# Keys and values of the fourth attention projected during the third feed-forward, four tiles at a time

## The reference

```
x = x + tanh(g_ffn[2])   * L2_ffn(layernorm(x))                  # the third feed-forward
x = x + tanh(g_xattn[3]) * L3_xattn(layernorm(x), ctx, ctx)      # the fourth attention

L2_ffn(x):     h = gelu(quant(x) @ quant(w_fc).T + b_fc)         # 128 -> 512, blocks of 32 share an exponent
               return quant(h) @ quant(w_proj).T + b_proj        # 512 -> 128
L3_xattn(q,k,v): q,k,v = q@Wq+bq, k@Wk+bk, v@Wv+bv               # 16 heads of 8
               return softmax(q k^T / sqrt(8)) v @ Wo + bo
```

## Time and profile before

| | |
|---|---|
| time, three runs | 1069.31, 1070.88, 1072.28 us; median 1070.88 |
| profiled execution | span 1084.4 us, 30129 instructions; no other time of it is given |
| busy | PE 898.7 us (83%), DVE 885.9 (82%), ACT 686.2 (63%), POOL 523.1 (48%) |
| mean granted PE clock | 0.898 |
| mask of attention 1 taken by DVE (L1896) | at 148.8 us |

### The profile page before, as it was taken

The page is one execution under the profiler, slowest core; times in us unless marked ns, Lnnn a source line. Parts: engine busy times, 40 slices in busy tenths (PEclk is TensorE's granted clock), DMA queues, the critical chain, the costliest instruction groups (busy, mean ns, idle before and its releaser), DMA issues.

```text
span 1084.4 us, 30129 instructions
## 1 busy us (share of the span) xinstructions
PE 898.7 (83%) x11539; PEld 707.4 (65%) x11557; DVE 885.9 (82%) x2296; ACT 686.2 (63%) x1794; POOL 523.1 (48%) x612
## 2 busy tenths in 40 slices
PE   8999999999999932999689999978899999434443
PEld 5888889978887721566457778834478888222222
DVE  6999888878999961567568889889978888899997
ACT  6888864377776610444447777866678888555553
POOL 6444412254367676223287787255553332355554
PEclk9999999999999966899889999988899999655665
DMA  8760000000000012365111111000000000000000
GB/s 214 186 241 2 3 2 2 1 2 3 3 24 27 27 46 76 114 187 175 51 33 32 26 31 29 6 1 2 1 2 2 2 3 3 1 10 16 15 15 24
DMA packets 60526, 44.42 MB, mean 41 GB/s; under 512 B 15196, under 2 KB 55781, under 8 KB 59366
## 3 DMA queue, kind: packets, MB, share of 16 engines
q1 hardware_dynamic: 55718, 34.09, 10.6%
q0 software_dynamic: 4096, 8.34, 2.7%
q10 hardware_dynamic: 576, 0.13, 0.1%
HBM read 23.73 MB, written 18.87 MB: 39 GB/s over the span
## 4 chain that ended last, share of the span: by engine, by line
PE 63%; DVE 21%; issue 6%; POOL 5%; ACT 2%; DVEq 2%; DMA 1%; POOLq 0%; another core or an unknown queue 0%; SPq 0%; ACTq 0%
PE ps L747 10%; PE ps L706 9%; PE ps L674 7%; PE ps L586 4%; PE ps L720 4%; PE ps L692 4%; POOL q_out L1232 3%; DVE rowmax L1879 3%; PE ps L782 3%; PE ps L791 3%; PE ps L783 3%; PE ps L640 2%; PE ps L655 2%; PE ps L653 2%; DVE sm L1885 2%
## 5 line engine op out<-in xcount | busy, mean ns | idle before, releaser
L1879 DVE TENSOR_REDUCE rowmax<-ps 128x16 f32<-128x1024 f32 x128 | 155.8, 1217 | 35.7 <-PE ps L674 34.4
L1885 DVE TENSOR_TENSOR sm<-ps,rowmax 128x512 f32<-128x512 f32 x256 | 164.9, 686 | 3.4
L1038 ACT ACTIVATE pr<-ps 128x512 f32<-128x512 f32 x256 | 138.9, 595 | 38.2 <-PE ps L747 36.0
L747 PE MATMUL ps<-cst,sm 128*128 128x128 f32 x1024 | 138.9, 277 | 13.3 <-DVE sm L1885 12.2
L706 PE MATMUL ps<-vbd,pr 128*64 128x18 f32 x4096 | 140.3, 211 | 0.5 <-ACT pr L1038 0.5
L706 PEld LDWEIGHTS ps<-vbd,pr 128*64 128x64 f32 x4096 | 134.2, 138 | 1.4 <-ACT pr L1038 1.3
L1320 POOL TENSOR_SCALAR xn<-x_sb,mv_all,rstd_all 128x128 f32<-128x128 f32 x122 | 98.2, 805 | 71.7 <-PE ps L640 65.7
L747 PEld LDWEIGHTS ps<-cst,sm 128*128 128x128 f32 x1024 | 112.8, 141 | 26.3 <-issue 19.5
L938 ACT ACTIVATE qbd<-ps,bqp,cst 128x128 f32<-128x128 f32 x256 | 104.6, 463 | 6.2 <-PE ps L655 2.4
L975 ACT ACTIVATE vbd<-ps 64x128 f32<-64x128 f32 x256 | 70.8, 277 | 34.2 <-PE ps L692 26.6
L1202 POOL DMA_INDIRECT big<-expert_out,row_g x64 | 68.2, 1066 | 49.9 <-DMA expert_out<-xn_all 22.8
(11 more groups left out here) (299 smaller groups left out, 2348.3 us busy)
## 6 DMA issues: line engine op xcount, KB each, us to landing
slots<-hT SPq DMA_DIRECT2D x8, 1024.0 KB, 11.0
sm<-slots SPq DMA_DIRECT2D x32, 256.0 KB, 3.3
expert_out<-xn_all SPq DMA_DIRECT2D x16, 256.0 KB, 3.0
ew<-in_L_ffn_w SPq DMA_DIRECT2D x24, 128.0 KB, 2.6
out<-x_sb SPq DMA_DIRECT2D x32, 64.0 KB, 1.5
slots<-xn_all,row_s POOLq DMA_INDIRECT x64
big<-expert_out,row_g POOLq DMA_INDIRECT x64
x_sb<-in_x SPq DMA_DIRECT2D x1, 512.0 KB, 4.6
```

Source lines behind the costliest of these rows:

```text
L747: last = nc.tensor.transpose(turned[b][:, r * P:(r + 1) * P], sm[x][:, c:c + P], ident)
L1038: nc.scalar.activation(pr[y][:, b, :], turned[b], ACT.Exp, scale=SCALE).then_inc(p_ready[y], 1)
L1879: v.tensor_reduce(row3, sc, AX.X, ALU.max).then_inc(rowmax_ready[x], 1)
L1885: v.tensor_tensor(sm[x][:, :].rearrange("p (r g k) -> p r g k", r=RG, k=S)[:, part], sc[:, part], row3[:, part].unsqueeze(3).broadcast_to( ...
```

## The change

Keys and values of attention 3 are made in feed-forward 2, in 16 sets: set 2g is the keys of tiles 4g to 4g+3 (one product of 512 columns), set 2g+1 their values (16 products of 64 columns). All go to `bank(1, 2)`, one after the other: a set waits until ACT has taken the one before (`ahead_kept`). Step 2 issues sets 0 and 1, step c from 3 to 16 set c-1. They stand where the second pair of idle products stood; the first pair, and those of the last steps, stay and now go to `bank(0, 2)`. ACT keeps the keys in `big` (two copies, as before with scale and bias, but of four tiles each) and the values in `xn_all` (one copy) at the end of the same step, after its GELU copies. In attention 3, PE makes only the queries, the scores read the keys from `big`, and ACT fills `vbd` from `xn_all` once the bank-free condition of the older tile (`o_psum`) holds. The two transposes of quantised inputs in feed-forward 2 go to one bank and are taken by one copy. Two semaphores are merged into others to make room for the two new ones: the mask's loads count on `blk_in`, and `scatters_late` on `pool_prep`.

```diff
+GROUP, GROUPS = 4, T // 4
...
+        keys3 = big[:, :].rearrange("p (t a k) -> p t a k", a=2, k=P)
+
+        def group(a, g):
+            return a[:, g * GROUP * P:(g + 1) * GROUP * P]
...
+            def value_products(l, t, dst):
+                for b in range(2):
+                    for a in range(2):
+                        cols = wv[l][:, :].rearrange("d (r a w) -> d a r w", a=2, w=2 * HD)[:, a, :, :]
+                        last = nc.tensor.matmul(dst[a * S:(a + 1) * S, b * S:(b + 1) * S].rearrange("p (r w) -> p r w", r=RG),
+                                                ctxT[:, t * P + b * S:t * P + (b + 1) * S], cols, start=True, stop=True, skip_group_check=True)
+                return last
+
+            def project_ahead(n):
+                if n > 0:
+                    pe.wait_ge(ahead_kept, n)
+                g = n // 2
+                if n % 2 == 0:
+                    nc.tensor.matmul(bank(1, 2), wk[3][:, :], group(ctxT, g), start=True, stop=True, skip_group_check=True).then_inc(ahead_psum, 1)
+                else:
+                    for t in range(GROUP):
+                        last = value_products(3, g * GROUP + t, bank(1, 2)[:, t * P:(t + 1) * P])
+                    last.then_inc(ahead_psum, 1)
...
-                    dst = bank_b(0, 0)[:, s * P:(s + 1) * P] if f == 1 else bank_b(s, 2)[:, 0:P]
+                    dst = bank_b(0, 0 if f == 1 else 2)[:, s * P:(s + 1) * P]
...
                     def key_and_query():
                         if ahead is not None:
-                            nc.tensor.matmul(project[:, 0:P], wk[l][:, :], ctxT[:, (t + 1) * P:(t + 2) * P], start=True, stop=True)
+                            if l != 3:
+                                nc.tensor.matmul(project[:, 0:P], wk[l][:, :], ctxT[:, (t + 1) * P:(t + 2) * P], start=True, stop=True)
...
+                        keys = keys3[:, t, :, :] if l == 3 else kT[x]
...
-                                                        kT[x][rows, :, b * S:(b + 1) * S], start=(l != 1), stop=True, skip_group_check=True)
+                                                        keys[rows, :, b * S:(b + 1) * S], start=(l != 1), stop=True, skip_group_check=True)
...
-                    if new is not None:
...
+                    if new is not None and l != 3:
+                        value_products(l, t, turned[1][:, 0:P]).then_inc(v_psum[x], 1)
...
-                        pe.wait_ge(v_taken[x], IT * l + new + 1)
+                        if l != 3:
+                            pe.wait_ge(v_taken[x], IT * l + new + 1)
...
                 if c > IT:
-                    keep_clock(6 * (c - IT))
+                    keep_clock(6 * (c - IT), bank(0, 2))
...
                 if px is not None and ph is not None:
-                    keep_clock(2)
+                    keep_clock(2, bank(0, 2))
...
-                    nc.tensor.matmul(bank(0, 1)[:, 0:P], wk[3][:, :], ctxT[:, 0:P], start=True, stop=True)
...
-                        pe.wait_ge(xnT_ready[s], IT * FFN2 + px + 1)
+                        pe.wait_ge(xnT_ready[NS - 1], IT * FFN2 + px + 1)
...
-                if px is not None and ph is not None:
-                    keep_clock(2)
+                for n in range(0 if c == 2 else c - 1, min(c, 2 * GROUPS)):
+                    project_ahead(n)
...
+            def keep_ahead(n):
+                act.wait_ge(ahead_psum, n + 1)
+                g = n // 2
+                if n % 2 == 0:
+                    for a in range(2):
+                        last = nc.scalar.activation(keys3[:, g * GROUP:(g + 1) * GROUP, a, :], bank(1, 2).rearrange("p (t k) -> p t k", k=P), ACT.Identity,
+                                                    scale=odd_pair[:, a:a + 1], bias=bkp[3][:, a:a + 1])
+                    last.then_inc(ahead_kept, 1)
+                else:
+                    nc.scalar.activation(group(xn_all, g), bank(1, 2), ACT.Copy).then_inc(ahead_kept, 1)
...
-                    if new is not None:
+                    if new is not None and l == 3:
+                        act.wait_ge(o_psum[x], IT * l + new)
+                        values(x, xn_all[:, t * P:(t + 1) * P])
+                    elif new is not None:
...
                 if px is not None:
                     act.wait_ge(quotients[0], c + 1)
                     hidden2(px)
+                for n in range(0 if c == 2 else c - 1, min(c, 2 * GROUPS)):
+                    keep_ahead(n)
...
-                        dve.wait_ge(mask_in, 32)
+                        dve.wait_ge(blk_in, 16 * 7)
```

More of the change, by code:

```diff
@@ L334, in flamingo @@
         x_first, late_in = sem("x_first"), sem("late_in")
-        attn_in, small_in, w0_in, blk_in, mask_in = (sem(n) for n in ("attn_in", "small_in", "w0_in", "blk_in", "mask_in"))
+        attn_in, small_in, w0_in, blk_in = (sem(n) for n in ("attn_in", "small_in", "w0_in", "blk_in"))
         dve_prep, pe_prep, act_prep, pool_prep = (sem(n) for n in ("dve_prep", "pe_prep", "act_prep", "pool_prep"))
@@ L348, in flamingo @@
         bst_ready = sems("bst_ready")
+        ahead_psum, ahead_kept = sem("ahead_psum"), sem("ahead_kept")
         s_psum, rowmax_ready, sm_ready, smT_psum, p_ready = (sems(n) for n in ("s_psum", "rowmax_ready", "sm_ready", "smT_psum", "p_ready"))
@@ L368, in flamingo @@
         got_in = [sems(f"got_in{p}_") for p in range(2)]
-        out_done, scatters_late = sem("out_done"), sem("scatters_late")
+        out_done = sem("out_done")
         block = stack.enter_context(nc.Block())
@@ L612, in lift_first @@
                 for s in range(NS):
-                    pe.wait_ge(xnT_ready[NS - 1 if k == FFN3 else s], IT * k + 1)
+                    pe.wait_ge(xnT_ready[NS - 1], IT * k + 1)
                     for n, w in enumerate(wide):
@@ L686, in half @@
                         pe.wait_ge(p_ready[y], 2 * (IT * l + prev) + 2)
-                    if new is not None:
-                        for b in range(2):
-                            for a in range(2):
-                                cols = wv[l][:, :].rearrange("d (r a w) -> d a r w", a=2, w=2 * HD)[:, a, :, :]
-                                dst = turned[1][a * S:(a + 1) * S, b * S:(b + 1) * S].rearrange("p (r w) -> p r w", r=RG)
-                                last = nc.tensor.matmul(dst, ctxT[:, t * P + b * S:t * P + (b + 1) * S], cols, start=True, stop=True, skip_group_check=True)
-                        last.then_inc(v_psum[x], 1)
+                    if new is not None and l != 3:
+                        value_products(l, t, turned[1][:, 0:P]).then_inc(v_psum[x], 1)
                     if oldest is not None:
@@ L793, in expert @@
                     last.then_inc(eo_psum[s], 1)
-            pe.wait_ge(scatters_late, 1)
+            pe.wait_ge(pool_prep, SCATTERS_LATE)
             keep_clock(26)
@@ L937, in key_and_query @@
                 for a in range(2):
-                    nc.scalar.activation(qbd[y][:, :, a], src[:, P:2 * P], ACT.Identity, scale=parity[:, a:a + 1], bias=bqp[l][:, a:a + 1])
+                    last = nc.scalar.activation(qbd[y][:, :, a], src[:, P:2 * P], ACT.Identity, scale=parity[:, a:a + 1], bias=bqp[l][:, a:a + 1])
+                if l == 3:
+                    last.then_inc(k_ready[y], 1)
+                    return
                 for a in range(2):
@@ L1002, in empty_quantised @@
                     act.wait_ge(xnT_psum[s], IT * k + px + 1)
-                    if k == FFN2:
-                        nc.scalar.activation(xqT[s], bank_b(s, 2)[:, 0:P], ACT.Copy).then_inc(xnT_ready[s], 1)
-                if k == FFN3:
-                    nc.scalar.activation(xqT_both[:, :, :].rearrange("d s p -> d (s p)"), bank_b(0, 0)[:, 0:NS * P], ACT.Copy).then_inc(xnT_ready[NS - 1], 1)
+                nc.scalar.activation(xqT_both[:, :, :].rearrange("d s p -> d (s p)"), bank_b(0, 2 if k == FFN2 else 0)[:, 0:NS * P], ACT.Copy
+                                     ).then_inc(xnT_ready[NS - 1], 1)
             def hidden2(px):
@@ L1378, in _ @@
                     if u == T - 2:
-                        pool.sem_inc(scatters_late, 1)
+                        pool.sem_inc(pool_prep, 1)
                     for c in range(2):
@@ L1899, in half @@
                         ffn0(0, 1, 0, 0, None, None)
-                        dve.wait_ge(blk_in, 16 * 5)
+                        dve.wait_ge(blk_in, 16 * 7)
                         v.tensor_reduce(w_max[:, :], w_blk[:, 2:5, :], AX.X, ALU.max, apply_absolute_value=True).then_inc(dve_prep, 1)
```

5 lines of the change are left out of this document (3 added, 2 removed).

## The result

The changed kernel takes 1068.54 us (median of 20 runs, 1067.03 to 1069.88); the kernel before, on the same chip, 1070.13 (20 runs, 1067.2 to 1075.91). The ratio is 0.9981 with an interval of 0.9973 to 0.9989: a gain of 2.0 us (1.2 to 2.9). The forecast was 1070.1 with a gain of 0.8, and no change beyond 0.3%. The profiled execution of the changed kernel took 1067.03 us, its span 1065.2.

The account below looks back on a forecast made before the run. PE was taken to bound the fourth attention, with a loop through DVE close behind. Terms -3.3 - 1.9 + 3.4 + 1.0 summed to -0.8 us, applied to the median: 1070.1, range 1065.8 to 1075.0.

Parts of the forecast that it names:

- forecast A: Whole kernel: the terms sum to -0.8 us, giving 1070.1, with its own range -2.6 to +1; chance 0.50.
- (1) Attention: Fourth attention: PE loses 0.60 us per tile, but tiles only fall from 4.12 to 4.01 us; gain 3.3 us.
- DVE loop: Fourth attention: DVE reduces and subtracts scores, PE turns them, then the single score banks are free; 4.01 us per tile.
- Rival E: Fourth attention: PE's whole 0.60 us per tile is gained, 17.4 us instead of 3.3, total 1056.0; chance 0.04.
- (2) Steady steps: Third feed-forward: low-clock stretches go, a pair of steps takes 9.7 us instead of 10.02; gain 1.9, bounds 0 and 2.3.
- rival B: Third feed-forward: low clock stays with the waits, start loses 5.1 us, steady steps gain nothing; +2.8, 1073.7; chance 0.15.
- D: Third feed-forward: rival that PE becomes the bound in even steps when low clock hits values; +5.8 us, 1076.7; chance 0.07.
- (3) Start: Feed-forward's first step: values wait for ACT's key copies until 717.3, next transposes 3.7 us late; loss 3.4, bounds 2.3 and 5.1.
- Rival C: Feed-forward's start: the late start is absorbed because the wait was not the last one; -4.2 us, 1066.7; chance 0.20.
- (4) End: Feed-forward's last steps: step 16's values ahead of idle products pass lateness to the attention; loss 1.0 us, bounds 0.5 and 1.1.
- (5) The rest: Merged transposes and copy, merged semaphores, POOL and DMA queues: nothing, bounds 0.1 us either way.

Follow-up runs that it names:

- before_again: The kernel before, unchanged, run once more for a second trace: 1075.77 us in its one run, span 1074.0.
- one_idle_product_per_tile: Changed kernel with one idle 512-column product ahead of the score transposes in each half of the fourth attention but the first: 1084.99 us, one run, second chip.
- sets_one_step_later: Changed kernel with set n issued in step n+2, never two per step, and 4 and 5 idle products ahead of steps 17 and 18: ratio 0.9934 to before.
- attention_only: Changed kernel without the product sets, idle pair restored; fourth attention makes no keys or values, so outputs differ: 1067.7 us, ratio 0.9958 to before.

## Why the prediction was right

The sum of the trace, -0.73 us, is the forecast's -0.8 almost to the digit, and the timed difference of 2.0 lies in forecast A's own range of -2.6 to +1. The mechanisms held, but the agreement to 0.1 us is luck: the four terms were off by -0.5, +0.3, +0.6 and -0.3 us, which cancel, and against before_again the same four stages give -2.4. Step by step:

**(1) Attention, -3.3; measured -3.82.** The step "the DVE loop stops it at 4.01" held: of PE's 0.60 us only 0.13 per tile came out. The term was 0.5 short because 4.01 was the distance of two early tiles, and the loop's own is 3.98; over 29 tiles that is 0.8 us, of which the forecast's roundings had taken in 0.3. Rival E fell with it, and one_idle_product_per_tile shows why. Two signs that the forecast named did not come: PE was to wait about half a microsecond per tile and to be busy near 88%, and it waits 0.24 ahead of the turned scores and counts as busy for 98%. Part of this is that 0.60 was too much: by the distances between starts the keys take 0.22 and the values 0.28 (857.07 to 857.35), 0.50 in all. The words "DVE loop" were loose: half the loop is PE's own turning and scores, during which DVE waits.

**(2) Steady steps, -1.9; measured -1.60 against the trace shown, -2.95 against before_again.** The pair of steps takes 9.71 us (9.7 was forecast), with no low clock, so rivals B and D fell here. The forecast's six pairs, steps 4 to 15, went from 60.10 to 58.24 us, -1.86; the table's -1.60 also holds step 16, which took 0.26 more. The kernel before has the same 4.76 and 4.96 us in those steps of before_again that hold no low stretch, so the gain here is that the low stretches are gone, and nothing else. The term's uncertainty is in the kernel before, not in the one after: 62.78 to 62.94 in five kernels with the sets and the idle pair, and 63.48 in a sixth, against 64.38 and 65.73 before. The priced bound that ACT's key copies might cost 0.2 per odd step did not come: 4.95 is what was forecast without it.

**(3) Start, +3.4; measured +3.97 (+3.65 against before_again).** The chain of waits held as written; where the low clock lay did not. From ACT's first GELU copy to the values the forecast had 717.3 - 714.75 = 2.55 us, the trace 698.80 - 696.33 = 2.47; from that copy to the transposes of step 3 6.35 was forecast, and 702.63 - 696.33 = 6.30 came. Inside the second stretch two errors cancelled. From the values to the transposes 3.8 us was forecast and 3.83 came (698.80 to 702.63), but the forecast had 2.7 for the values, three quarters of them at the low clock, and 1.1 for bias rows and idle products at the full one: it left the low stretch where it had been. In the trace the values are through in 1.83 (698.80 to 700.63) and the rest takes 2.00, as it did before: the values were priced too high, and the low stretch came later than taken. It is as long as before, 6.8 us, but begins 6.05 us behind step 2's block maxima (692.85 to 698.90) instead of 1.5 (711.27 to 712.8), after the wait and not in it. The second error is also what was left over: step 3's own products were to run 0.2 to 0.3 us faster than before, and they ran at the low clock too (0.50 until 705.7), from the transposes to step 4 in 4.19 us instead of 3.86. So the loss is 3.97 and not 3.4. Rival C fell: nothing absorbed the late start, and sets_one_step_later, which has no such wait, is 4.0 us shorter in this stage.

So of rival B the mechanism came true in this one step, and its price did not: with everything up to the transposes at the low clock it had 717.3 + 3.04 + 2.2, 7.8 us from the GELU copies, where 6.30 came. After 0.71 us of work in 3.4, PE made the values in 1.90 us, and the same 32 instructions take 1.15 at full clock. The Trainium skill, "TensorE: Matmul & The Clock Gate", section "HAM oscillation — how this bites in real kernels", says that a burst behind a long wait starts cold; the trace agrees for this wait. In the changed kernel's steady steps there is no such wait, and the clock stayed at 1.00. But a long wait is not the only thing that goes before a fall: in the kernel before the clock fell in steady steps where PE's longest wait was 0.7 us (725 to 785, clock 0.83).

**(4) End, +1.0; measured +0.72.** Mechanism right, price high. The values of four tiles were taken at 1.52 us from 0.38 a tile; in the stream they are 1.08, and 1.08 - 0.43 = 0.65. By the forecast's own count the 1.0 came all the same: the transposes of step 17 stand 5.97 us behind the block maxima of step 16 (765.06) instead of 4.96. Of that 1.01 the values with the idle products behind them make 0.67, and 0.35 is that step 16's values begin 3.27 us behind those maxima, where the idle products began at 2.92. Here are step 16's values, the idle products behind them, and the transposes of step 17 that stand late:

```profile
768.33 1.15 PE L522 MATMUL ps<-wv,ctxT 128*64 128x64 f32 x32
769.64 1.24 PE L516 MATMUL ps<-amask,ones_b 128*128 128x512 bf16 x5 [0.16 <-issue]
...
771.03 0.62 PE L891 MATMUL ps<-ident_b,q_out 128*128 128x128 bf16 x8
```

The same too high price made the even steps look tighter than they are: PE waits 0.24 to 0.33 us for POOL's lowered quotients in every steady step, so D was further off than its row prices said.

**(5) The rest, 0.** No run takes it out alone; every changed kernel has it. For the one copy and the other bank, attention_only speaks: its start and end are before_again's within 0.02 us. For the mask the second attention speaks, 153.0 us in before_again and in the four changed kernels traced at the same pace. The merged `scatters_late` is open: the experts' stage, from the second attention's last row maxima to the third's first, takes 173.7 us in before_again and 171.6 to 172.7 in those four; at the slower pace it takes 175.5 in the trace shown of before and 174.2 to 175.6 in the other four.

What was not seen: the base. One trace of the kernel before has 10.00 and 64.38 us where another has 10.32 and 65.73, and a sum of four terms of 1 to 4 us was set against the kinder of the two. That is the likely reason why the timed gain is 1.2 us larger than the forecast; the experts' stage is another, and no run separates them. The gain is clear of zero, 1.2 to 2.9 us, and below the 0.3% that the forecast named.

## What to carry to other kernels

Work taken off a full engine is worth only the distance to the next loop; look for that loop in the first and last tiles of a stage, where the full engine has less to do, and average it over several of them. Read the engine's waits from distances between starts, or put a known product in: here PE counted as busy for 98 and 100% of a loop that it did not bound. Work moved into an engine's idle time needs its hand-over checked at both ends: here 5.4 us were gained in the stages' middles and 4.7 given back in one first step that had two sets for one bank, and in one last step whose idle products had already filled the wait; one set per step, with fewer idle products at the end, took both away. Where a stage has a clock that falls now and then, take two traces of the kernel before as the base, not one.

## What the runs showed that was not expected

The third attention, whose code is the same in every kernel here, took 134.8 to 135.4 us in five traces and 146.6 to 148.2 in five others, among them all four of the second chip. Its POOL, grouped by line over that stage, first in the trace shown of before and then in that of the changed kernel:

```profile
L1202 POOL DMA_INDIRECT big<-expert_out,row_g x54 | 57.9, 1072 | 24.6 <-issue 13.4 <-PE ps L674 11.2
```

```profile
L1243 POOL DMA_INDIRECT big<-expert_out,row_g x54 | 58.5, 1084 | 13.1 <-issue 13.1
```

The 54 gathers cost the same; in the slower pace POOL also stands 11.2 us for PE's scores. What makes a chip fall into the one or the other stays open. The two chips' medians of the kernel before lie 15.2 us apart, of which the third attention makes about 12; at the slower pace the second attention (154.4 against 153.0 us) and the experts' stage are longer too. It moves no verdict, since each ratio is taken on one chip.

Two prices: a product of 512 f32 columns (two records in the trace) is followed by the next instruction 0.91 us later (781.30 to 782.21 in sets_one_step_later), about four of the 0.22 that a tile's 128 columns took; 16 products of 64 f32 columns (32 records) take 1.08 (739.21 to 740.29 after), 0.27 per tile, where the chain gave a tile's in the attention 0.38 and the distance between starts 0.28. A share of a chain is not the price of the same instructions in a stream.
